# Three 16-bit products in place of one 32-bit product for the projections of the first attention, in a four-layer kernel on one core

## The reference, cut to what matters

```python
x = x + _L0_xattn_ref(_layernorm(x), ctx_1024, mask_BxSxS2_bk0, position_bias, Wq, Wk, Wv, Wo)

def _L0_xattn_ref(query, key_value, mask, position_bias, Wq, Wk, Wv, Wo):
    # 8 batches, 256 queries, 256 keys, width 128, 16 heads of 64
    hq, hk, hv = (a @ W.T for a, W in ((query, Wq), (key_value, Wk), (key_value, Wv)))  # 128 -> 16 x 64
    score = einsum('bhqd,bhkd->bhqk', hq, hk) / sqrt(64) + position_bias
    probs = softmax(where(mask, score, -inf), axis=-1)   # 0 where masked
    return einsum('bhqk,bhkd->bhqd', probs, hv) @ Wo.T
```

## Time and profile before

| | |
|---|---|
| median of 3 runs | 1648.45 us (1639.2 to 1649.18) |
| time of the profiled execution | 1648.66 us |
| its span | 1646.9 us |
| `wide_attention`, batch 0's jobs to its last `out` | about 31.5 to 391 us |
| PE busy over the span | 1393.0 us (85%) |
| DVE, ACT, POOL busy | 978.4 (59%), 889.0 (54%), 781.8 us (47%) |

### The profile page before, as it was taken

The page is one execution under the profiler, slowest core; times in us unless marked ns, Lnnn a source line. Parts: engine busy times, 40 slices in busy tenths (PEclk is TensorE's granted clock), DMA queues, the critical chain, the costliest instruction groups (busy, mean ns, idle before and its releaser), DMA issues.

```text
span 1646.9 us, 37117 instructions
## 1 busy us (share of the span) xinstructions
PE 1393.0 (85%) x14303; PEld 863.7 (52%) x14394; DVE 978.4 (59%) x2412; ACT 889.0 (54%) x1455; POOL 781.8 (47%) x690
## 2 busy tenths in 40 slices
PE   3899999994599999999598988678585995999948
PEld 2466666663477777777343443334463553444425
DVE  4677777773444444443588888455755334666753
ACT  2677777762299999999244444212232222555512
POOL 4677777763199999999332322100602003344200
PEclk9999999996699999999799999679695996999968
DMA  8000000003100000000101010000000000000000
GB/s 257 8 8 8 8 8 9 1 2 113 38 26 17 23 26 26 26 26 15 61 30 59 30 36 20 1 1 19 9 3 1 1 0 10 8 8 5 2 1 26
DMA packets 25639, 39.96 MB, mean 24 GB/s; under 512 B 6884, under 2 KB 12936, under 8 KB 24872
## 3 DMA queue, kind: packets, MB, share of 16 engines
q1 hardware_dynamic: 24936, 36.10, 6.7%
q0 software_dynamic: 576, 2.10, 0.6%
HBM read 39.24 MB, written 1.05 MB: 24 GB/s over the span
## 4 chain that ended last, share of the span: by engine, by line
PE 66%; DVE 16%; issue 11%; ACT 3%; POOL 2%; SPq 1%; DMA 1%; POOLq 0%; DVEq 0%; ACTq 0%
PE bank L2059 10%; PE bank L2047 10%; PE bank L1345 4%; DVE sbuf L1455 4%; PE bank L2260 3%; PE bank L1698 3%; PE bank L1283 3%; PE bank L1767 2%; PE bank L1748 2%; DVE sbuf L1472 2%; PE bank L2246 2%; PE bank L1788 2%; PE bank L1702 2%; DVE sbuf L320 2%; PE bank L1299 2%
## 5 line engine op out<-in xcount | busy, mean ns | idle before, releaser
L2030 POOL TENSOR_TENSOR sbuf<-sbuf 128x512 f16<-128x512 f32 x256 | 307.0, 1208 | 63.9 <-ACT sbuf L2085 62.2
L2085 ACT ACTIVATE sbuf<-bank,sbuf 128x512 f32<-128x512 f32 (+1 forms) x512 | 317.0, 698 | 15.8 <-PE bank L2047 6.5
L2059 PEld LDWEIGHTS bank<-sbuf 128*128 128x128 f16 x3072 | 192.7, 98 | 59.5
L2059 PE MATMUL bank<-sbuf 128*128 128x128 f16 x3072 | 212.7, 219 | 0.0
L2047 PE MATMUL bank<-sbuf 128*128 128x512 f16 x768 | 208.4, 381 | 2.9 <-DVE sbuf L2097 2.9
L1455 DVE TENSOR_REDUCE sbuf<-bank 128x4 f32<-128x1024 f32 x128 | 156.3, 1221 | 76.6 <-PE bank L1299 65.7
L326 POOL TENSOR_TENSOR sbuf<-sbuf 128x16 f32<-128x16 f32 x8 | 23.3, 2908 | 375.8 <-DVE sbuf L316 375.8
L2107 DVE SCALAR_TENSOR_TENSOR sbuf<-bank,sbuf 128x128 f32<-128x128 f32 x256 | 71.9, 343 | 188.6 <-PE bank L2059 188.6
L1252 POOL TENSOR_TENSOR sbuf<-sbuf 128x512 f16<-128x512 f32 x64 | 66.6, 1040 | 239.0 <-ACT sbuf L1397 239.0
L1668 POOL TENSOR_TENSOR sbuf<-sbuf 128x512 f16<-128x512 f32 x128 | 147.9, 1176 | 65.9 <-ACT sbuf L1847 65.7
L1345 PE MATMUL bank<-sbuf 128*32 128x256 f32 x2048 | 140.9, 395 | 0.8 <-ACT sbuf L1417 0.8
(11 more groups left out here) (234 smaller groups left out, 2691.4 us busy)
## 6 DMA issues: line engine op xcount, KB each, us to landing
sbuf<-w SPq DMA_DIRECT2D x32, 256.0 KB, 2.7
sbuf<-bias_t SPq DMA_DIRECT2D x4, 1024.0 KB, 15.3
sbuf<-ctx_t SPq DMA_DIRECT2D x24, 128.0 KB, 2.5
sbuf<-bias_q POOLq DMA_DIRECT2D x4, 512.0 KB, 14.8
sbuf<-mask_t SPq DMA_DIRECT2D x8, 256.0 KB, 2.7
sbuf<-bias_t SPq DMA_DIRECT2D x8, 256.0 KB, 3.1
sbuf<-mask_q SPq DMA_DIRECT2D x8, 256.0 KB, 3.6
sbuf<-bias_q SPq DMA_DIRECT2D x8, 256.0 KB, 4.2
```

The lines of the kernel that those rows point to most:

```text
L2030: g.tensor_tensor(hid16[1][:, u % BUFS, :], hid[:, u % 4, :], hid16[0][:, u % BUFS, :], ALU.subtract)\
L2059: last = pe.matmul(bank[4 + out_no % 2][:, j * P:(j + 1) * P], hid16[h][:, u % BUFS, j * P:(j + 1) * P], w2_16[p][:, w, f * D:(f + 1) * D] ...
L2085: last = act.activation(to, bank[u % 4][:, :], ACT.Gelu, bias=b1[u // U][:, u % FT0:u % FT0 + 1], scale=1 / SCALE)
```

## The change

Queries, keys and values are projected by three 16-bit matmuls for each 32-bit one. VectorE makes the 16-bit halves: of the three weight tiles once, scaled by 256 (ScalarE's copies divide by it), and of the normed input and the context once for each batch (`operands(b)`: two casts and two subtractions of 128x256). Batches 0 and 1 are halved ahead of the units, batch b + 1 in unit 0 of batch b, between VectorE's `weigh` and `scores`. The jobs move from units 0, 1, 2, 5, 6, 7 to units 2 to 7. The weights now land in tiles of the exponentials and are waited for by VectorE; `wo` has a semaphore of its own and is loaded a little later.

```diff
@@ wide_attention @@
-            JOBS_AT = ((0, 1), (2, 3), (4, 5), (), (), (6, 7), (8, 9), (10, 11))
+            JOBS_AT = ((), (), (0, 1), (2, 3), (4, 5), (6, 7), (8, 9), (10, 11))
...
+            wq, wk0, wv = (take([2, 1024], F16) for _ in range(3))
+            xs16, cs16 = ([take([2, S], F16) for _ in range(2)] for _ in range(2))
+            loaded = (exps[:, 0, :], exps[:, 1, :], biased[:, 0, :])
+            PASSES = ((0, 0), (0, 1), (1, 0))
+            SCALE = 2.0 ** 8
...
                     if b >= 2:
-                        sp.wait_ge(s["projected"], (b - 2) * JOBS + JOBS)
+                        sp.wait_ge(s["operands"], b - 1)
                     sp.dma_start(ctx_t[b % 2], io["ctx_t"][:, b * S:b * S + S]).then_inc(ctx_in[b % 2], 16)
...
                 contexts(1)
+                sp.dma_start(wo, io["wo0"]).then_inc(wo_in, 16)
...
-                pe.wait_ge(w0_in, 64)
-                pe.wait_ge(nrm_xt, normed)
+                pe.wait_ge(s["weights"], 3)
...
                     if k == 0:
-                        pe.wait_ge(ctx_in[b % 2], b // 2 * 16 + 16)
+                        pe.wait_ge(s["operands"], b + 1)
...
-                        for c in range(2):
+                        for c, (n, (w, a)) in product(range(2), enumerate(PASSES)):
                             m = 2 * pair + c
-                            last = pe.matmul(to[:, c * S:(c + 1) * S], (wq, wk0)[kind][:, m * P:(m + 1) * P],
-                                             ct if kind else xt, start=True, stop=True)
+                            last = pe.matmul(to[:, c * S:(c + 1) * S], (wq, wk0)[kind][:, w, m * P:(m + 1) * P],
+                                             (xs16, cs16)[kind][b % 2][:, a, :], start=n == 0, stop=n == 2)
                     else:
                         t, hf = divmod(k - QK, 2)
-                        last = pe.matmul(to[:, :], ct[:, t * P:(t + 1) * P], wv[:, hf * 512:(hf + 1) * 512],
-                                         start=True, stop=True)
+                        for n, (a, w) in enumerate(PASSES):
+                            last = pe.matmul(to[:, :], cs16[b % 2][:, a, t * P:(t + 1) * P],
+                                             wv[:, w, hf * 512:(hf + 1) * 512], start=n == 0, stop=n == 2)
...
                 def out(b, m):
+                    if b == m == 0:
+                        pe.wait_ge(wo_in, 16)
...
-                    scale = DH0 ** -0.5 if k < QK and k % 2 == 0 else 1.0
+                    scale = (DH0 ** -0.5 if k < QK and k % 2 == 0 else 1.0) / SCALE
...
             def vector(v):
                 c = dve(v)
-                v.wait_ge(w0_in, 64)
+
+                def operands(b):
+                    v.wait_ge(ctx_in[b % 2], b // 2 * 16 + 16)
+                    v.wait_ge(nrm_xt, normed - CHUNKS + b // 2 + 1)
+                    wait(v, s["projected"], (b - 1) * JOBS)
+                    xt = xn_t[:, b * S:b * S + S]
+                    v.tensor_copy(cs16[b % 2][:, 0, :], ctx_t[b % 2])
+                    c.step(v.tensor_copy(xs16[b % 2][:, 0, :], xt)).settle()
+                    v.tensor_tensor(cs16[b % 2][:, 1, :], ctx_t[b % 2], cs16[b % 2][:, 0, :], ALU.subtract)
+                    v.tensor_tensor(xs16[b % 2][:, 1, :], xt, xs16[b % 2][:, 0, :], ALU.subtract).then_inc(s["operands"], 1)
+
+                v.wait_ge(w0_in, 48)
+                for w, to in zip(loaded, (wq, wk0, wv)):
+                    c.step(v.tensor_scalar(to[:, 0, :], w, SCALE, None, ALU.mult)).settle()
+                    v.scalar_tensor_tensor(to[:, 1, :], w, SCALE, to[:, 0, :], ALU.mult, ALU.subtract).then_inc(s["weights"], 1)
+                operands(0)
                 c.step(v.memset(parts, 0.0)).settle()
                 c.step(v.memset(part_of[:, :, :, 2], -LIFT)).settle()
+                operands(1)
...
                     weigh(u)
+                    if b + 1 < B and n == 0 and b:
+                        operands(b + 1)
                     if u + AHEAD < UNITS:
                         scores(u + AHEAD)
```

More of the change, by code:

```diff
@@ L1525, in wide_attention @@
             s = {k: sem("w0_" + k) for k in (
+                "weights",
+                "operands",
                 "projected",
@@ L1548, in wide_attention @@
             mask_in = [sem(f"w0_mask_in{p}") for p in range(2)]
+            wo_in = sem("w0_wo_in")
             x0 = x_steps[0]
@@ L1572, in wide_attention @@
             shift = take([2, S], BF16)
-            wq, wk0, wv, wo = take([1024]), take([1024]), take([1024]), take([PAIRS, D])
+            wq, wk0, wv = (take([2, 1024], F16) for _ in range(3))
+            wo = take([PAIRS, D])
+            xs16, cs16 = ([take([2, S], F16) for _ in range(2)] for _ in range(2))
+            loaded = (exps[:, 0, :], exps[:, 1, :], biased[:, 0, :])
+            PASSES = ((0, 0), (0, 1), (1, 0))
+            SCALE = 2.0 ** 8
             bias_t = take([H, HW])
@@ L1635, in sync @@
                 contexts(0)
-                for tile, name in ((wq, "wq0"), (wk0, "wk0"), (wv, "wv0"), (wo, "wo0")):
+                for tile, name in zip(loaded, ("wq0", "wk0", "wv0")):
                     sp.dma_start(tile, io[name]).then_inc(w0_in, 16)
@@ L1689, in project @@
                     if k == 0:
-                        pe.wait_ge(ctx_in[b % 2], b // 2 * 16 + 16)
+                        pe.wait_ge(s["operands"], b + 1)
                     to = pr_bank("job", b, k)
-                    xt = xn_t[:, b * S:b * S + S]
-                    ct = ctx_t[b % 2]
                     if k < QK:
                         pair, kind = divmod(k, 2)
-                        for c in range(2):
+                        for c, (n, (w, a)) in product(range(2), enumerate(PASSES)):
                             m = 2 * pair + c
-                            last = pe.matmul(to[:, c * S:(c + 1) * S], (wq, wk0)[kind][:, m * P:(m + 1) * P],
-                                             ct if kind else xt, start=True, stop=True)
+                            last = pe.matmul(to[:, c * S:(c + 1) * S], (wq, wk0)[kind][:, w, m * P:(m + 1) * P],
+                                             (xs16, cs16)[kind][b % 2][:, a, :], start=n == 0, stop=n == 2)
                     else:
                         t, hf = divmod(k - QK, 2)
-                        last = pe.matmul(to[:, :], ct[:, t * P:(t + 1) * P], wv[:, hf * 512:(hf + 1) * 512],
-                                         start=True, stop=True)
+                        for n, (a, w) in enumerate(PASSES):
+                            last = pe.matmul(to[:, :], cs16[b % 2][:, a, t * P:(t + 1) * P],
+                                             wv[:, w, hf * 512:(hf + 1) * 512], start=n == 0, stop=n == 2)
                     last.then_inc(s["projected"], 1)
```

## The result

The changed kernel takes 1667.54 us in the median of 4 runs (1661.5 to 1674.07), the kernel before 1646.09 (1639.2 to 1649.18) beside it: 21.5 us slower, ratio 1.0137 with a 95% interval of 1.0085 to 1.0189. The forecast was 1644 with a range up to 1667, so the sign is wrong and the time lies just past the end. Rival (c) comes nearest: the clock fell in each of the six batches and the operands took 5.0 us where 2.8 were counted.

A forecast was written before the change was run, and what follows sets the result against it. TensorE was taken to set the pace. Batch 0 saves 4.0 us, batches 1 to 6 keep 5.4, the start loses 4.7: 4.7 us faster than 1648.7, so 1644, range 1630 to 1667.

The forecast's parts named there:

- Rival (c): TensorE's clock halves behind the hole in units 0 and 1: 1656 to 1665 us, up to 1676; chance 0.26.
- What bounds the kernel: Steady part of the stage: TensorE sets the pace, busy for 38.49 of 40 us, the other engines 29 to 31.
- the chain in units 0 and 1: Batches 1 to 6: VectorE's operands delay scores and cut, TensorE waits ahead of `maxima`; 3.1 us lost a batch.
- x + 0.3: Loss in us per batch in units 0 and 1 of batches 1 to 6, forecast as 2.8 + 0.3 = 3.1.
- x: Length of VectorE's four operands operations in unit 0: forecast 2.8 us, from 1.25 if free to 5.1 if all wait.
- The jobs: Projection matmuls: 0.65 us a set, 0.33 saved for a job, TensorE's queue 4.0 us shorter in batches 0 to 6.
- The step that failed first: Operands in unit 0: two of four operations wait for GpSimd, whose leftover work ends near 4.3 us; x = 2.8.
- The step that failed second: Clock in units 0 and 1 of batches 1 to 6: expected at 1.00, no loss in the sum.
- Start: Ahead of the first jobs: halving weights and first operands delays TensorE to 36.3; 4.7 us lost, bounds 3.6 to 6.2.
- The sum: Whole kernel: 4.0 saved in batch 0, 5.4 in batches 1 to 6, 4.7 lost at start: 4.7 us faster.

The follow-up runs named there:

- run 3: Changed kernel with 20 filler matmuls of 512 columns ahead of TensorE's wait for the cut in unit 1 of batches 1 to 6: median 1659.91 us.
- Run 2: Changed kernel with GpSimd's subtractions cut to 2 columns in units 7 and 0, one head in job 11's split: median 1633.48 us.
- run 9: Changed kernel with the two casts done early, behind unit 3, and only the two subtractions left in unit 0: median 1657.7 us.
- run 1: Changed kernel without the halving in the loop; batches 2 to 7 use the halves of batches 0 and 1: median 1634.79 us.
- run 5: Changed kernel with operands halved two batches ahead, casts behind VectorE's work of unit 3, subtractions behind unit 4: median 1640.38 us.

## Why the prediction was wrong, point by point

- **What bounds the kernel, and the chain in units 0 and 1: right.** The stall is x + 0.3 by the prediction; with x = 5.0 that is 5.3, and run 3 measures 5.0 over units 0 and 1, 5.2 over the batch (43.71 less the 38.5 below). Run 2 gives 3.36 + 4.58 - 6.64 = 1.3 for x = 1.29, so the 0.3 is not there. TensorE waits where it was said, ahead of `maxima` for the cut.
- **The jobs: right in kind, a little large.** 0.65 us a set. TensorE's own work for a batch is 38.5 us (3.36, the 3.14 of the earlier trace rows, 4.86, 6.62, 6.64, 4.52, 4.83, 4.56), 3.7 less than 42.19 where 4.0 was forecast; batch 0 gave 2.9.
- **The step that failed first: "I count the first two operations as waiting, ... and the last two as free: x = 2.8."** All four waited, x = 5.0. The end of the range had it (5.1, from the medians in the earlier trace rows); the value was taken near the other end by the argument that GpSimd has only one or two pieces left. Two were left when the first operation began, as it said. But each wait pushed VectorE's next operation back, and the leftover work ended 5.0 us after TensorE's start of unit 0, not 4.3, right where unit 0's own `low` put two more pieces: four pieces for four operations. Run 2 shows that GpSimd is the whole of the difference, 1.29 against 5.0. This costs 2.2 us a batch, 13 in all.
- **The step that failed second: the clock, left to rival (c).** The forecast's sum has nothing for it. It fell in all six batches, which is 7.8 us by run 3; run 9 shows that it would have fallen at the forecast's own x. Rival (c) had the mechanism but priced a fall too high, 2 to 3.5 us a batch where 1.0 to 2.2 were measured. Its "up to 1676" is also low by its own terms: 1665 and six times 2.3 us more of x are 1679. That the time still came out just past the range is luck: a larger x and a cheaper fall of the clock made up for each other.
- **Start: a term mis-sized.** 4.7 forecast with bounds of 3.6 to 6.2, 3.4 measured at the first weigh. TensorE's start was right within 0.3 us (36.04 for 36.3), and ScalarE's is 3.9 later than before, as forecast. Behind it nothing more was lost, where up to 1.9 had been allowed for: from ScalarE's start to the first weigh it is 20.3 us (37.52 to 57.86), before 20.9 (33.59 to 54.45).
- **What was missed: the cut can wait for GpSimd too.** Its two operations took 1.75 us in run 1 where the kernel before has 0.41: there the cut began at 5.2 us of the unit, when GpSimd was nearly done (5.4), in run 1 at 4.4, and GpSimd works until 7.3. In batches 1 to 6 of the changed kernel it does not show (0.18 and 0.19 us), since the operands had held the cut back behind GpSimd's work. In batch 7 it does (0.60 and 1.16): units 0 and 1 take 3.36 + 4.76 = 8.12 us in place of 3.58 + 3.68 = 7.26, 0.9 more, and run 2, with GpSimd quiet, has 7.26 again. That is about half of the 1.7 us lost behind batch 6.
- **The sum, made again** with what was measured: start +3.4; batch 0 -2.9; six batches of 38.5 + 5.2 + 1.3 = 45.0 against 42.19, +16.9; batch 7 and tail +1.7: 19.1 slower, against 4.7 faster forecast. The medians say 21.5; the 2.4 us between are within what the unchanged stages scatter (6 us between the two profiled executions). Of the 23.8 us between forecast and sum, 13 are x and 7.8 the clock.
- The rule of the Trainium skill that the prediction cited ("SBUF — State Buffer", "SBUF: two separate sides": an exclusive turn for a whole instruction) is borne out here by 1.2 to 1.4 us where 0.28 to 0.43 are the operation's own; the prediction named it and then let only two of the four operations wait.

## What to carry to other kernels

Beside a busy GpSimd, the casts and subtractions of this kernel with all operands in SBUF, and the two operations of the cut, ended only behind a piece of GpSimd's work: one piece (1.1 to 1.2 us) for each operation of a row, however small the operation (0.58 and 1.17 us for 128x8, 1.2 to 1.4 for 128x256). Price each of a row so, not the first alone. Count GpSimd's pieces on to the end of the row with its waits in it, and look for the place where another engine's work covers it, or give it to GpSimd's own queue (2.2 us there, 5.0 us on VectorE here). Work moved out of a stretch takes its cover away: the same four operations cost nothing in units of 6.6 us (run 5) and 5 us in units of 3.4 and 3.1. A stall of TensorE can cost more than its length: 4.9 us cost 1.0 to 2.2 us more in half clock, and behind 2.66 to 2.96 us the clock fell too.

## What the runs showed that was not expected

- Operations of 128x8 wait for GpSimd like those of 128x256 (0.58 and 1.17 us in run 1), while `reciprocal`, of 128x4, took 0.18 us each time beside the same GpSimd work. Why they differ no run shows.
- The clock fell behind holes of 2.66 to 2.96 us (run 9) and held at 1.00 in runs 1 and 2, where the hole at the same place is 1.34 and 1.16 us.
- How much a fall costs differs from batch to batch in one execution (1.0 to 2.2 us), while with the clock held all six batches are equal within 0.02 us (43.70 to 43.72).
